# Another order for the first norm, the first kernel K and the first projection of a state-space stage

## The reference, cut to what matters

```python
mod = (_silu(L0_c) @ L0_wmod).reshape(L0_c.shape[0], 6, 1, -1)   # and the same for L1
ga = (2 * (ga >= 0) - 1) * jnp.maximum(jnp.abs(ga), 0.25)
h = _layernorm(x, axis=-1) * (1 + ca) + sa                      # x: 2048 tokens of 128
x = x + ga * s4(h)

# one of the four layers of s4, h as 128 channels x 2048 tokens
z = _layernorm_channels(h, ln_w[i], ln_b[i])
dt = jnp.exp(log_dt); A = -jnp.exp(A_re_log) + 1j * A_im; dtA = A * dt[:, None]
C = (C_re + 1j * C_im) * (jnp.expm1(dtA) / A)
K = 2.0 * jnp.einsum('hn,hnl->hl', C, jnp.exp(dtA[:, :, None] * l)).real
y = causal_convolution(z, K) + z * D_skip[:, None]              # written with FFTs there
y = jax.nn.gelu(y)
out = jnp.einsum('oh,bhl->bol', W, y) + bvec[None, :, None]
h = out[:, :H] * jax.nn.sigmoid(out[:, H:]) + h
```

## Time and profile before

| | us |
|---|---|
| median of 3 executions | 1254.43 |
| lowest and highest | 1253.78, 1258.54 |
| the profiled execution | 1254.49 |
| its span, first to last instruction | 1252.7 |
| TensorE, VectorE busy | 990.9, 776.8 |
| ScalarE, GpSimd busy | 526.5, 430.1 |
| mean granted clock of TensorE, share of full | 0.883 |

### The profile page before, as it was taken

The page is one execution under the profiler, slowest core; times in us unless marked ns, Lnnn a source line. Parts: engine busy times, 40 slices in busy tenths (PEclk is TensorE's granted clock), DMA queues, the critical chain, the costliest instruction groups (busy, mean ns, idle before and its releaser), DMA issues.

```text
span 1252.7 us, 19990 instructions
## 1 busy us (share of the span) xinstructions
PE 990.9 (79%) x7944; PEld 677.4 (54%) x7944; DVE 776.8 (62%) x1344; ACT 526.5 (42%) x1211; POOL 430.1 (34%) x453
## 2 busy tenths in 40 slices
PE   2669788878254389999999777769879898979888
PEld 2456466565232277878787652334456644546643
DVE  6656457564757234646464669869946656956654
ACT  4635656445025121212212060016677725768642
POOL 4373524313007300000000124528934334954420
PEclk9686777979586589999999878979989999979999
DMA  3007451717113574445431220000022210012101
GB/s 103 1 1 146 84 96 36 139 41 140 26 54 160 107 120 85 100 100 98 103 76 25 80 83 0 1 0 1 1 52 52 65 67 26 1 35 53 36 17 34
DMA packets 60719, 76.55 MB, mean 61 GB/s; under 512 B 37740, under 2 KB 42232, under 8 KB 58872
## 3 DMA queue, kind: packets, MB, share of 16 engines
q1 hardware_dynamic: 60636, 75.41, 26.7%
HBM read 52.92 MB, written 1.51 MB: 43 GB/s over the span
## 4 chain that ended last, share of the span: by engine, by line
PE 51%; DVE 17%; POOL 14%; ACT 7%; issue 5%; DMA 4%; SPq 1%; POOLq 0%; DVEq 0%
PE psum L1288 7%; PE psum L1290 7%; PE psum L1289 7%; POOL rest L1540 3%; POOL rest L1530 3%; POOL rest L1536 2%; PE psum L766 2%; PE psum L1783 2%; PE psum L1776 2%; ACT rest L1474 2%; PE psum L791 2%; PE psum L1829 2%; DMA rest<-share_d 2%; POOL rest L1566 2%; DVE main L1630 1%
## 5 line engine op out<-in xcount | busy, mean ns | idle before, releaser
L427 POOL TENSOR_TENSOR kept<-kept 128x8 f32<-128x8 f32 x8 | 1.6, 204 | 370.2 <-DVE kept L388 370.2
L1474 ACT ACTIVATE rest<-psum,main 128x128 f32<-128x128 f32 x256 | 113.4, 480 | 11.5 <-POOL main L1551 8.9
L1135 ACT ACTIVATE x_high<-main 128x512 fp32r<-128x512 f32 x48 | 30.3, 633 | 199.6 <-DVE main L1209 199.6
L1288 PE MATMUL psum<-x_high,w_low 128*128 128x512 f32 x192 | 77.0, 401 | 20.0 <-DVE x_low L1214 20.0
L1566 POOL TENSOR_TENSOR rest<-rest,main 128x512 f32<-128x512 f32 x64 | 65.4, 1044 | 45.5 <-DVE main L1636 45.5
L1289 PE MATMUL psum<-x_low,w_high 128*128 128x512 f32 x192 | 76.4, 398 | 0.0
L1290 PE MATMUL psum<-x_high,w_high 128*128 128x512 f32 x192 | 76.3, 397 | 0.0
L1288 PE MATMUL psum<-hid_high,w_low 128*128 128x512 f32 x192 | 75.6, 394 | 0.7 <-DVE main L1233 0.7
L1209 DVE TENSOR_TENSOR main<-kept,rest 128x512 f32<-128x512 f32 x48 | 33.0, 690 | 68.5 <-PE psum L1290 43.9
L1289 PE MATMUL psum<-hid_low,w_high 128*128 128x512 f32 x192 | 74.8, 389 | 0.0
L1290 PE MATMUL psum<-hid_high,w_high 128*128 128x512 f32 x192 | 74.7, 389 | 0.0
(11 more groups left out here) (332 smaller groups left out, 2784.9 us busy)
## 6 DMA issues: line engine op xcount, KB each, us to landing
rest<-share_d SPq DMA_DIRECT2D x4, 3072.0 KB, 21.0
rest<-share_d SPq DMA_DIRECT2D x4, 2304.0 KB, 20.4
main<-main SPq DMA_DIRECT2D x32, 256.0 KB, 6.1
main<-k_pad SPq DMA_DIRECT2D x16, 512.0 KB, 8.1
rest<-main SPq DMA_DIRECT2D x32, 256.0 KB, 3.5
main<-w_dram SPq DMA_DIRECT2D x2, 3072.0 KB, 13.3
main<-rest SPq DMA_DIRECT2D x32, 128.0 KB, 2.3
rest<-tables_dram SPq DMA_DIRECT2D x2, 2048.0 KB, 9.2
```

What stands on the lines that cost most here:

```text
L1288: T.matmul(dst, w_small, x_large, start=first, stop=False)
L1474: last = A.activation(probs[:, p, 4 * r + m, :], bank[2 * p + r][:, m * P:(m + 1) * P], ACT.Exp, scale=row_scale[:, c, r, m:m + 1], bias=r ...
```

## The change

- VectorE: the residues become a function of their own behind near turns 0. `centre` and the statistics of the first norm come ahead of near turns 0, the modulation's small instructions behind the residues, then the normed tokens, the norm's output, far turns 0, powers 0, and near turns 1. Near turns 2 move from the start of layer 0 to behind the rotation.
- TensorE: the tokens' transposes come ahead of the modulation, which has bank 7. In the first channel norm the variances and z of blocks 0 and 1 come ahead of all of `back`. K(0) leaves its place ahead of the projection and now follows the projection, near angles 2 and far angles 1; K(1) has bank 2. `exponents(2)` come ahead of K(1). Of `back(1)` ten groups come ahead of y and six behind it, in banks 4 and 5, with a wait for their copies ahead of the gate matmuls. Behind each later channel norm stand four matmuls whose result nobody reads.
- ScalarE: `back` 0 to 3 ahead of squares 2 and 3, the rest behind; the roundings of near2 and far1 ahead of K(0)'s rows; magnitudes 2 ahead of `back(1)`.
- GpSimd waits for all of `consts_in`, to which the two rows of powers now belong; far0 no longer waits for the modulation; near1 and exp1 follow `ln_pool` and `weighted`; the decay of layer 0 comes behind them, that of a later layer behind the coefficients.
- SyncE issues `cond` ahead of `ident` and `xT`.

```diff
--- before.py
+++ after.py
@@ -402,8 +402,7 @@
...
-        def ln_dve_alone(dve, n, normed, dst, scale, bias, between):
-            ln_dve_stats(dve, n)
+        def ln_dve_normed(dve, n, normed):
             for b in range(BLOCKS):
@@ -412,7 +411,8 @@
...
                 last.then_inc(sem("ln_normed" if b < 2 else "ln_normed_late"), 1)
-            between()
...
+        def ln_dve_out(dve, n, dst, scale, bias):
             for b in range(BLOCKS):
@@ -456,10 +456,16 @@
...
         CENTRED, SCORED = ((0, 1, 0, 1), (0, 1, 2, 3)), ((2, 3, 2, 3), (7, 5, 4, 6))
-        TURNED_BACK = ((6, 7), (1, 3), (1, 3), (1, 3))
-        GATED, GATE, KERNEL = (4, 6), 5, (5, 0, 0, 0)
         BACKS = HG // 2
-        NEAR_FIRST, FAR_FIRST = (4, 4, 4, 0), (0, 6, 6, 6)
+        EARLY = (BACKS, 10, 10, 10)
...
+        def turned_back(N, q):
...
+            pair = ((6, 7), (1, 0), (1, 3), (1, 3))[N] if N != 1 or q < EARLY[1] else (4, 5)
+            return bank[pair[q % 2]]
...
+        GATED, GATE, KERNEL = (4, 6), 5, (0, 2, 0, 0)
+        NEAR_FIRST, FAR_FIRST = (4, 4, 4, 0), (0, 2, 6, 6)
         PRODUCT = {name: n + 1 for n, name in enumerate(("near2", "far1", "exp2", "near3", "far2", "exp3", "far3"))}
@@ -470,6 +476,10 @@
...
+        def s4_dve_residues(dve, link):
...
+            V = nc.vector
             V.tensor_tensor(square4, exps4[:, :, 1, :], exps4[:, :, 1, :], ALU.mult)
@@ -582,7 +592,6 @@
...
             if L == 0:
-                s4_dve_near_turns(dve, 2)
                 dve.wait_ge(sem("s4_dta"), 2)
@@ -600,6 +609,7 @@
...
             if L == 0:
+                s4_dve_near_turns(dve, 2)
                 s4_dve_far_turns(dve, 1)
@@ -681,15 +691,13 @@
...
-        EARLY = (BACKS, BACKS, 10, 10)
...
                 for i in range(4):
-                    last = nc.tensor.transpose(bank[TURNED_BACK[N][q % 2]][0:CHUNK, i * P:(i + 1) * P], (pow_re, pow_im)[i % 2][N % 2][:, 2 * q + i // 2, :], ident)
+                    last = nc.tensor.transpose(turned_back(N, q)[0:CHUNK, i * P:(i + 1) * P], (pow_re, pow_im)[i % 2][N % 2][:, 2 * q + i // 2, :], ident)
                 last.then_inc(sem("s4_back_ps"), 1)
@@ -726,22 +734,20 @@
...
             s4_pe_centre(pe, 0, 1)
-            pe.wait_ge(sem("s4_pow"), 3)
-            s4_pe_back(pe, 0, range(4))
             s4_pe_var(pe, 0, 0)
...
             s4_pe_z(pe, 0, 1)
-            s4_pe_back(pe, 0, range(4, 8))
+            pe.wait_ge(sem("s4_pow"), 3)
+            s4_pe_back(pe, 0, range(4))
             s4_pe_centre(pe, 0, 2)
             s4_pe_centre(pe, 0, 3)
-            s4_pe_back(pe, 0, range(8, 10))
+            s4_pe_back(pe, 0, range(4, 8))
             s4_pe_var(pe, 0, 2)
...
             s4_pe_z(pe, 0, 3)
-            s4_pe_back(pe, 0, range(10, BACKS))
-            s4_pe_kernel(pe, 0)
+            s4_pe_back(pe, 0, range(8, BACKS))
@@ -767,8 +773,14 @@
...
             if L == 0:
+                s4_pe_near_angles(pe, 2)
+                pe.wait_ge(sem("s4_in"), 1)
+                s4_pe_far_angles(pe, 1)
+                s4_pe_kernel(pe, 0)
                 pe.wait_ge(sem("s4_turns"), ANGLE["near2"])
-                s4_pe_far_angles(pe, 1)
+                s4_pe_exponents(pe, 2)
+                pe.wait_ge(sem("s4_turns"), ANGLE["far1"])
+                pe.wait_ge(sem("s4_k_rows"), 1)
             if L and L + 2 < S4_LAYERS:
@@ -776,10 +788,6 @@
...
                 s4_pe_back(pe, L + 1, range(EARLY[L + 1]))
-            if L == 0:
-                pe.wait_ge(sem("s4_turns"), ANGLE["far1"])
-                s4_pe_exponents(pe, 2)
@@ -803,6 +811,8 @@
...
                 s4_pe_back(pe, L + 1, range(EARLY[L + 1], BACKS))
+            if L == 0:
+                pe.wait_ge(sem("s4_back"), 2 * BACKS)
@@ -823,12 +833,14 @@
...
                 s4_pe_z(pe, N, 3)
+                for _ in range(4):
+                    nc.tensor.matmul(bank[0][:, :], centre, hT[:, 0:512], start=True, stop=True)
             else:
...
             A = nc.scalar
-            act.wait_ge(sem("s4_prm_in"), 48)
+            act.wait_ge(sem("s4_prm_in"), 16)
             A.activation(exps4, prm4[:, :, 0:2, :], ACT.Exp).then_inc(sem("s4_rates"), 1)
@@ -898,7 +910,7 @@
...
                 act.wait_ge(sem("s4_back_ps"), N * BACKS + q + 1)
-                nc.scalar.activation(back[:, 2 * q:2 * q + 2], bank[TURNED_BACK[N][q % 2]][0:CHUNK, :].rearrange("p (a b c) -> p a b c", a=2, b=2),
+                nc.scalar.activation(back[:, 2 * q:2 * q + 2], turned_back(N, q)[0:CHUNK, :].rearrange("p (a b c) -> p a b c", a=2, b=2),
                                      ACT.Copy).then_inc(sem("s4_back"), 1)
@@ -934,16 +946,14 @@
...
                 s4_act_sines_near(act, L + 2)
-            if L == 0:
-                s4_act_round_far(act, 1)
             if L and ahead:
...
                 s4_act_sines_far(act, L + 1)
+                if L == 0:
+                    s4_act_magnitudes(act, 2)
                 s4_act_back(act, L + 1, range(EARLY[L + 1]))
                 s4_act_k_rows(act, L + 1)
-            if L == 0:
-                s4_act_magnitudes(act, 2)
             A.activation(warm[:, 3 * L + 2:3 * L + 3], warm[:, 0:1], ACT.Gelu_apprx_tanh)
@@ -1064,11 +1074,11 @@
...
-            s4_pool_decay(pool, L)
             if more:
...
                     s4_pool_coefficients(pool, chain, L + 2)
+                s4_pool_decay(pool, L + 1)
                 s4_pool_weighted(pool, L + 1)
@@ -1887,10 +1897,10 @@
...
                 src = bass.AP(tensor=first_row, offset=offset, ap=[[0, P], [1, size]])
-                sp.dma_start(powers_of[:, at:at + size], src).then_inc(sem("s4_prm_in"), 16)
+                sp.dma_start(powers_of[:, at:at + size], src).then_inc(sem("consts_in"), 16)
+            sp.dma_start(cond, dram["cond"]).then_inc(sem("consts_in"), 16)
             sp.dma_start(ident, dram["ident"]).then_inc(sem("consts_in"), 16)
             sp.dma_start(xT, dram["xT"]).then_inc(sem("x_in"), 16)
-            sp.dma_start(cond, dram["cond"]).then_inc(sem("consts_in"), 16)
             sp.dma_start(sel, dram["sel"]).then_inc(sem("consts_in"), 16)
@@ -1967,16 +1977,18 @@
...
             chain.link(nc.gpsimd.memset(neg_half, -0.5))
+            pool.wait_ge(sem("consts_in"), 96)
             pool.wait_ge(sem("s4_dta"), 1)
...
             s4_pool_outer(pool, outer_exp[0], 0, 0, near_powers)
-            pool.wait_ge(sem("cond"), 3)
             s4_pool_outer(pool, outer_far, 0, 1, far_powers)
+            ln_pool(pool, LN_A)
+            s4_pool_weighted(pool, 0)
             s4_pool_outer(pool, outer_near[1], 1, 1, near_powers)
-            ln_pool(pool, LN_A)
             s4_pool_outer(pool, outer_exp[1], 1, 0, near_powers)
-            s4_pool_weighted(pool, 0)
+            pool.wait_ge(sem("s4_rates"), 2)
+            s4_pool_decay(pool, 0)
             s4_pool_norm(pool, 0)
@@ -2008,7 +2020,7 @@
...
             s4_act_rates(act)
-            act.wait_ge(sem("consts_in"), 64)
+            act.wait_ge(sem("consts_in"), 96)
             nc.scalar.activation(cond_sig, cond, ACT.Sigmoid).then_inc(sem("cond"), 1)
@@ -2021,12 +2033,13 @@
...
             s4_act_square(act, 0, 1)
-            s4_act_back(act, 0, range(8))
+            s4_act_back(act, 0, range(4))
             s4_act_square(act, 0, 2)
             s4_act_square(act, 0, 3)
-            s4_act_back(act, 0, range(8, BACKS))
+            s4_act_back(act, 0, range(4, BACKS))
+            s4_act_round_near(act, 2)
+            s4_act_round_far(act, 1)
             s4_act_k_rows(act, 0)
-            s4_act_round_near(act, 2)
             for L in range(S4_LAYERS):
@@ -2051,19 +2064,24 @@
...
             V.tensor_tensor(cond_silu, cond, cond_sig, ALU.mult).then_inc(sem("cond"), 1)
+            dve.wait_ge(sem("consts_in"), 96)
+            V.tensor_scalar(centre, ident, 1.0 / P, None, ALU.subtract)
+            ln_dve_stats(dve, LN_A)
             s4_dve_near_turns(dve, 0)
+            s4_dve_residues(dve, link)
             dve.wait_ge(sem("cond"), 3)
-            link(V.tensor_copy(mod, bank[3][:, 0:12]))
+            link(V.tensor_copy(mod, bank[7][:, 0:12]))
             V.tensor_scalar(mod_sign, mod, 0.0, 2.0, ALU.is_ge, ALU.mult)
...
             link(V.tensor_scalar(mod_abs, mod_abs, 0.25, None, ALU.max))
-            V.tensor_scalar(centre, ident, 1.0 / P, None, ALU.subtract)
             V.scalar_tensor_tensor(gate, mod_sign, -1.0, mod_abs, ALU.add, ALU.mult).then_inc(sem("cond"), 1)
+            ln_dve_normed(dve, LN_A, z_tok)
             dve.wait_ge(sem("cond"), 4)
+            ln_dve_out(dve, LN_A, hT, one_plus[:, 1:2], mod[:, 0:1])
             s4_dve_far_turns(dve, 0)
-            ln_dve_alone(dve, LN_A, z_tok, hT, one_plus[:, 1:2], mod[:, 0:1], lambda: s4_dve_near_turns(dve, 1))
             s4_dve_powers(dve, 0)
+            s4_dve_near_turns(dve, 1)
             dve.wait_ge(sem("to_dram"), 16)
@@ -2078,24 +2096,20 @@
...
             T = nc.tensor
-            pe.wait_ge(sem("consts_in"), 64)
```

(11 more changed lines are left out.)

## The result

| | before | changed |
|---|---|---|
| median, us | 1254.07 | 1243.51 |
| lowest and highest | 1252.73, 1258.54 | 1238.69, 1245.96 |
| profiled execution (its span) | 1254.49 (1252.7) | 1245.96 (1244.2) |
| granted clock, mean | 0.883 | 0.883 |

The changed kernel took 0.9906 of the time before, with a 95% interval of 0.9883 to 0.993. The profiled execution is the slowest of the five; the medians are over five executions of each.

A forecast was written before the change was run, and what follows sets the result against it. The prediction took TensorE to hold 51% of the chain of waits, with the early chain on VectorE until 43.3 us. Terms 10.4 - 3.3 + 3.0 - 3.3 = +6.8 us on 1254.43 gave 1261, range 1246 to 1268.

The forecast's parts named there:

- The start (+10.4): Layer 0's beginning up to the first squares: these come at 62.5 us, 10.4 later than before.
- the sign: Whole kernel: slower by 6.8 us; chances 0.45 slower, 0.36 within 0.5%, 0.19 faster by more.
- I take 1.64: First norm: each GpSimd power blocks VectorE's small instructions for its whole 1.64 us; bounds 0 and 1.64.
- the convoy: Beginning: about ten small VectorE instructions wait behind GpSimd's three long ones, VectorE through at 37.3 us; forecast's chance 0.52.
- rival 1: Beginning: VectorE gets through before GpSimd reaches near1, done at 27; squares at 54.5, total 1253 us; chance 0.22.
- The price that I named for the move: Beginning: near turns 1 come only behind powers 0, ending at 53.7 us where they ended at 43.33 before.
- From the squares to y (S+87): Layer 0: y starts 87 us after the first squares S, at 149.5; before it was S+90.3; gain 3.3.
- Behind y (+3.0, bounds 1 and 4): Layer 0, y to gate: six late groups back and two roundings on ScalarE cost 3.0 us.
- The dummies (-3.3, bounds 0 and -7.5): Projections of layers 1 to 3: dummies keep the full clock into part of each, saving 1.1 us three times.
- rival 2: The convoy as forecast, but dummies hold the full clock through every projection: 7.6 for 3.3 us, 1257; chance 0.10.
- The decay (nothing): GpSimd's decay moved behind the coefficients costs nothing, since scans need it only twenty us later.

The follow-up runs named there:

- e6: Changed kernel with GpSimd's outer product near1 ahead of the first norm's powers, against the changed kernel; 1251.71 us, a single run.
- e5: Changed kernel with VectorE's far turns 0 ahead of the normed tokens and near turns 1 ahead of the norm's output; 1234.42 us, 0.9862 of the kernel before.
- e7: The changed kernel itself, unaltered, measured and profiled a second time; 1245.5 us, 0.9931 of the kernel before.
- e9: Changed kernel without the dummy matmuls and with the decay of layers 1 to 3 at its old place; 1254.3 us, 0.9995 of the kernel before.
- e1: Changed kernel without its four dummy matmuls behind each channel norm; 1251.15 us, 0.9966 of the kernel before.
- e2: Changed kernel with the decay of layers 1 to 3 back behind GpSimd's copies of z; 1249.86 us, 0.996 of the kernel before.
- e10: The kernel of e5 with VectorE's residues moved behind the norm's output too; 1237.42 us, 0.9861 of the kernel before.
- e11: The kernel of e5 with all sixteen groups back(1) ahead of y; 1235.53 us, 0.9854 of the kernel before.
- e4: The kernel before with only the dummy matmuls and the decay's move added; 1245.82 us, 0.9918 of the kernel before.
- e8: The kernel before with only the decay's move added; 1249.16 us, 0.9968 of the kernel before.
- e3: Changed kernel with all sixteen groups back(1) ahead of y; 1243.59 us, 0.9906 of the kernel before.

## Why the prediction was wrong, step by step

**The start (+10.4): failed, and with it the sign.** The failed step is "I take 1.64": that the powers hold VectorE's residues. Shown by L492 and L493 inside L431 at 0.29, and by e6, where an outer product held the same L483 for 3.70. I had bounds of 0 and 1.64 a power and chose the upper, by the name of the form; the convoy of ten small instructions behind near1 never formed. The squares came at 51.70, 0.45 earlier than before; near turns 1 started at 40.60 and not at 51.4. My rival 1 had this mechanism but put the squares at 54.5. That was a slip within the sum: the same terms that lead from 37.3 to 62.5 lead from its own 27 to 52.2. I had also read L475 too widely: in the same timeline before, L476, a reciprocal with one SBUF input, took 0.95 us inside the second outer product (12.36 to 13.31), and 0.95 in the changed kernel with no outer product beside it. The price that I named for the move, near turns 1 behind powers 0, is real: e5 takes it back and gains another 0.4 to 0.7%.

The rule that I weighed there (the Trainium skill, SBUF — State Buffer, Who interferes with whom: whoever has the shared port pair keeps it for the whole instruction) holds for the outer product, 3.70 against 0.28. For a power of 128x8 the trace disagrees, 0.29 beside 1.69, and the measurement decides: the lock, if it is one, wasn't held through that instruction.

**From the squares to y (S+87): right in sum.** Measured S+86.3; before S+90.3. The projection came at S+24.2 (I: 25.4). Coefficients(1) took 108.36 to 121.56, 13.2 us for my 15 and 5.55 undisturbed. GpSimd's timeline in the changed kernel, which answers to the coefficients of the earlier trace rows:

```profile
109.03 2.05 POOL L1023 TENSOR_TENSOR rest<-rest 128x32 f32<-128x32 f32 x1
111.16 1.27 POOL L1024 TENSOR_TENSOR rest<-rest 128x32 f32<-128x32 f32 x1
...
117.11 1.26 POOL L1029 TENSOR_TENSOR rest<-rest,main 128x32 f32<-128x32 f32 x1
118.34 0.25 POOL L1030 TENSOR_TENSOR rest<-rest 128x32 f32<-128x32 f32 x1
```

For seven instructions (L1023 to L1029) a quarter of a microsecond became 1.1 to 2.05 while VectorE had its scans and products, and went back to 0.25 behind them. With a start right as well, y would have been forecast at 138.7; it came at 137.99.

**Behind y (+3.0, bounds 1 and 4): mis-sized.** From the start of y to the first gate it was 14.3 us before and 22.5 in the changed kernel (e7: 22.7), +8.2. ScalarE's copies of the six groups (154.48 to 159.1) are 4.6, where I had 3.9 for them less what other work would cover; the other 3.6 are largely the near and far angles at 1.2 GHz, 6.41 + 3.62 us. In e9, with the six groups but near angles at full clock, the distance was 18.8, +4.5. Why the clock falls so early behind y in the changed kernel, in both its profiles, and in e6, but not in e1, e2, e5, e9 and e10, stays open. One thing goes with it: the gap inside y is 1.26 to 1.43 us in the first three and 0.90 to 1.10 in the others. It isn't the whole of it, since e11 has a gap of 1.54 and its near angles took 4.08.

**The dummies (-3.3, bounds 0 and -7.5): right in kind, sized too small.** In the traces, from VectorE's last z copy to the rotation, the layers were 1.4, 1.6 and 2.1 us shorter, 5.1. By the runs they are worth 4.4 (e2 against e9), 6.3 (e4 against e8) and 4.4 or 7.5 (the changed kernel's two ratios against e1). I had argued that the full clock would last into a part of the projection; it lasted through 181 to 184 and, by the mean of 0.73 over the next window, to some 185.4 of 186.4 (my estimate). This was one half of rival 2, to which I gave one in ten; the other half, the convoy, didn't happen. My argument against it (the projection never raised the clock in 7 us) was no argument: what holds a clock that is up need not raise one that is down. Nor was the 2.1 us after the last matmul, which I had read the earlier trace rows, a fixed time: in e9, with the same idle stretch of 4.9 us and no dummies, the clock fell 4.4 us after it.

**The decay (nothing): failed.** I asked who needs the decay's result, and not which of VectorE's instructions ran beside it. The row of the long copy, 3.44, was in the trace before; the projection's release by L550 stood in the earlier trace rows. By the runs it is worth 4.0 (e8), 3.6 (e1 against e9) and 3.6 or 6.8 us (the changed kernel's two ratios against e2).

**The sum.** In the traces: 4.5 earlier at y, 8.2 later behind it, 5.1 for the dummies, 4.9 for the copies, so -6.3; the span has -8.5, and 2 us are not assigned to an edit. They belong to the beginning: from the first gate to gate 3, e9 took 200.4 us for 202.4 before, with neither edit at the borders, and the changed kernel 190.3. In the runs the parts add up: the beginning 0.9995, the decay 0.9968, both edits at the borders 0.9918, all 0.9906 or 0.9931. With the borders at e4's -10.3 and the start as forecast it would have come to about 0, with the start right and the borders as forecast to about -4, both within 0.5%: it took both errors to say "slower". The term behind y was too small by 5.2 us as well and hid part of them.

## What to carry to other kernels

When an instruction of GpSimd is moved, look at both places for the VectorE instruction beside it, above all one that releases TensorE: a copy at twice its length is the sign, and it recurs in every layer. A change that makes an early milestone earlier is worth only what arrives at the next shared one, here the gate; follow it there before it is counted. Where two bounds of an unseen pairing decide the sign, forecast both cases with nearly equal chances rather than choose an end by the name of the instruction.

## What was not expected of the hardware

- A GpSimd power over 128x8 (1.64 to 1.77 us) didn't slow VectorE's 128x128 instructions with two SBUF inputs (0.28 to 0.29); a product over 128x2048 held one for 3.59 and one for 3.70 us (e6).
- Four dummy matmuls, 3.6 us in all, ahead of small 64x32-tile matmuls kept these at 2.4 GHz (the first 180 of 256 in 2.57 us, clock 1.00), which alone never raised it: in the kernel before they took 7.05 us, at 0.50 throughout.
- TensorE was busy for all of 146 to 150 (4.00 us) with the 32-row matmuls L662 and L670, and the granted clock was 0.50, 1.2 GHz, throughout.
- Most series of small matmuls that ran at the full clock have a gap of 0.6 to 1.7 us put down to "issue" (142.11, 184.68; 182.13 in e2). It stands behind the same matmul each time, the 180th of layer 1's projection in the changed kernel, e2, e3, e5 and e7. The projections of layers 1 to 3 at 1.2 GHz, of before and of e1, have none. So part of what the clock gives is lost there; the cause wasn't tried.
